# Four chained graph layers on one core: bf16 digits, a tanh, more count buffers and two sweeps reordered

## The reference

```
att   = (q[dst] * kt[edge_type, src]).sum(-1) * mu / sqrt(32)
alpha = segment_softmax(att, dst)
agg   = segment_sum(vt[edge_type, src] * alpha, dst)
out   = typed_linear(gelu(agg), Wa, ba, node_type)      # gelu in its tanh form
x     = a * out + (1 - a) * x
```

## Time and profile before

| | us |
|---|---|
| median of 3 runs | 10061.57 (10060.24 to 10063.58) |
| profiled execution | 10059.76, of which the span is 10058.0 |
| POOL busy | 6847.6 |
| DVE busy | 5828.1 |
| ACT busy | 3071.7 |
| PE busy | 1997.3 |

### The profile page before, as it was taken

One profiled execution on the slowest core, in us unless ns is written; L12 is line 12 of the kernel. 1 busy time (PEld: TensorE's weight loads), 2 busy tenths in 40 slices (PEclk: granted clock), 3 DMA queues, 4 the chain that ended last, 5 costly groups with the idle time before them and its releaser, 6 DMA issues. The chain is left out here.

```text
span 10058.0 us, 59982 instructions
## 1 busy us (share of the span) xinstructions
PE 1997.3 (20%) x16162; PEld 1843.8 (18%) x16162; DVE 5828.1 (58%) x9520; ACT 3071.7 (31%) x3309; POOL 6847.6 (68%) x7186
## 2 busy tenths in 40 slices
PE   4555465651000000002500008000022000110002
PEld 3555465551000000002500007000022000100002
DVE  8777565553545554556588886788874322432225
ACT  6333143331223332232354543355431000110002
POOL 2777777777777777775477763677734777667773
PEclk9999955555555555556855558555555555555556
DMA  3511011111333333334466655566642333223332
GB/s 95 208 29 28 24 44 33 33 31 53 98 99 114 113 109 105 108 110 139 166 212 213 215 183 172 187 217 209 217 124 65 107 103 107 87 90 107 103 107 58
DMA packets 490844, 1161.90 MB, mean 116 GB/s; under 512 B 184121, under 2 KB 279692, under 8 KB 432396
## 3 DMA queue, kind: packets, MB, share of 16 engines
q0 software_dynamic: 255936, 474.70, 18.1%
q1 hardware_dynamic: 204620, 628.82, 16.6%
q10 hardware_dynamic: 29952, 54.54, 2.1%
HBM read 669.61 MB, written 487.92 MB: 115 GB/s over the span
## 5 line engine op out<-in xcount | busy, mean ns | idle before, releaser
L832 POOL DMA_INDIRECT slots<-REC,plc_idx x1664 | 1597.9, 960 | 554.3 <-issue 505.6
L1238 POOL DMA_INDIRECT l_swp_G<-table,KVI x1664 | 1573.3, 945 | 529.1 <-issue 506.3
L940 POOL DMA_INDIRECT l_G<-table,OTHI x1664 | 1581.6, 951 | 513.3 <-issue 506.2
L1490 POOL DMA_INDIRECT l2s_G<-table,OTHI x832 | 785.0, 944 | 428.9 <-issue 253.3
L1490 POOL DMA_INDIRECT l3s_G<-table,OTHI x832 | 786.2, 945 | 301.6 <-issue 253.3
L703 PEld LDWEIGHTS plc_pr<-plc_seen,plc_otf 128*128 128x128 f32 x3328 | 848.4, 325 | 21.3 <-issue 12.1
L703 PE MATMUL plc_pr<-plc_seen,plc_otf 128*128 128x49 f32 x3328 | 849.9, 410 | 11.1 <-DVE plc_seen L618 11.0
L1073 DVE TENSOR_TENSOR l_LB<-l_RE,l_G 128x64 f32<-128x64 f32 x104 | 29.4, 282 | 1024.7 <-DMA l_G<-table,OTHI 1024.5
L1340 DVE SCALAR_TENSOR_TENSOR l_swp_QS<-l_swp_QS,KEEP,l_swp_QX 128x128 f32<-128x128 f32 x1664 | 588.4, 354 | 36.0 <-DMA l_swp_QX<-queries 8.3
L1099 DVE TENSOR_TENSOR_SCAN l_X<-l_AW,l_X 128x2244 f32<-128x2244 f32 x104 | 502.5, 4831 | 3.6
L1399 DVE TENSOR_TENSOR_SCAN l_swp_X<-l_swp_AW,l_swp_X 128x2244 f32<-128x2244 f32 x104 | 501.4, 4821 | 0.1
(11 more groups left out here) (491 smaller groups left out, 9751.1 us busy)
## 6 DMA issues: line engine op xcount, KB each, us to landing
sums<-l_ROW SPq DMA_DIRECT2D x104, 1088.0 KB, 4.3
sums<-l_swp_ROW SPq DMA_DIRECT2D x104, 1088.0 KB
l_swp_QX<-queries SPq DMA_DIRECT2D x104, 1024.0 KB, 7.8
queries<-plc_zrow SPq DMA_DIRECT2D x33, 1664.0 KB
sums<-l3s_ROW SPq DMA_DIRECT2D x52, 1032.0 KB, 4.3
plc_low<-low_rows ACTq DMA_DIRECT2D x208, 256.0 KB, 3.4
sums<-l2s_ROW SPq DMA_DIRECT2D x52, 1024.0 KB, 4.4
table<-t_row SPq DMA_DIRECT2D x98, 512.0 KB
```

What stands on the lines that cost most here:

```text
L832: pool.indirect_dma_start(out=slots, out_offset=bass.IndirectOffsetOnAxis(ap=idx[:, c % IB, j:j + 1], axis=0), in_=g.REC[:, c * CH + j, :] ...
L940: pool.indirect_dma_start(out=G[:, c % GR, j, :], out_offset=None, in_=table, in_offset=bass.IndirectOffsetOnAxis(ap=g.OTHI[:, side(c), x: ...
L1238: pool.indirect_dma_start(out=G[:, c % GR, j, :], out_offset=None, in_=table, in_offset=bass.IndirectOffsetOnAxis(ap=index[:, c * CK + j:c ...
L1490: pool.indirect_dma_start(out=G[:, c % GR, j, :], out_offset=None, in_=table, in_offset=bass.IndirectOffsetOnAxis(ap=g.OTHI[:, k, c * CK + ...
```

## The change

Five things change.

1. The digits are stored as bf16 with the low digits of a key in one run and the high ones in another (`DIG[key, half, column]`), and a f32 copy of the low digits, `LOW`, is kept for ACT and for the transposes. The one-hot tiles are stored with the columns of a chunk interleaved by four, so that the innermost run of `compare` is four neighbours in both inputs and the output. The iota it reads is stored with each value four times (`iota_s` in SBUF, `iota_p` in PSUM). PE and ACT read and write single columns of the tiles with a stride of four values.
2. `count_keys` has 8 buffers, and ACT takes one chunk of four instead of one of three.
3. The gelu is 0.5 x (1 + tanh(z)): Tanh on ACT in the place of Exp, one product on DVE; the 0.5 is put into the weight once.
4. In the attention sweep each half of a chunk's gathers has its own semaphore, and `weigh`, `add_up` and `carry` of the last chunk but one are done in its own iteration.
5. In layer 0's sweep `add_up(c)` and `rows_of(c)` are done in iteration c, behind the pieces of other work.

```diff
+IN = 4
+OB = 8
 def compare(v, out, iota, number):
-    full = [P, out.shape[1], out.shape[2]]
-    return v.tensor_tensor(out, iota.rearrange("p (o w) -> p o w", o=1).to_broadcast(full),
-                           number.to_broadcast(full), ALU.is_equal)
+    full = [P, CH // IN, out.shape[2], IN]
+    return v.tensor_tensor(out, iota.rearrange("p (o w i) -> p o w i", o=1, i=IN).to_broadcast(full),
+                           number.rearrange("p (q o i) -> p q o i", o=1, i=IN).to_broadcast(full), ALU.is_equal)
...
-            v.tensor_copy(down_b[:, :], down[:, 0:1].to_broadcast([P, P]))
+            for to in (cuts, g.iota_s):
+                v.tensor_copy(to[:, 0:IN * P].rearrange("p (w i) -> p w i", i=IN),
+                          g.iota[:, :].rearrange("p (w i) -> p w i", i=1).to_broadcast([P, P, IN]))
...
-                v.tensor_copy(g.DIG[:, k, :, 0], lo[:, :])
-                link(v.tensor_copy(g.DIG[:, k, :, 1], hi[:, :]))
+                v.tensor_copy(g.DIG[:, k, 0, :], lo[:, :])
+                v.tensor_copy(g.LOW[:, k, :], lo[:, :])
+                link(v.tensor_copy(g.DIG[:, k, 1, :], hi[:, :]))
...
+def column(digits, j):
+    return digits[:, j // IN, :, j % IN]
...
-            for c in range(2, NCH, 3):
-                if c >= 3:
-                    act.wait_ge(counted, c - 2)
+            for c in range(3, NCH, 4):
+                if c >= OB:
+                    act.wait_ge(counted, c - OB + 1)
                 for x in range(CH):
-                    o = act.activation(olo[:, 2, x, :], g.iota_b[:, :], ACT.Square, scale=-1.0,
-                                       bias=g.DIG[:, k, c * CH + x, 0:1])
+                    o = act.activation(column(olo[:, c % OB, :, :, :], x), g.iota_b[:, :], ACT.Square, scale=-1.0,
+                                       bias=g.LOW[:, k, c * CH + x:c * CH + x + 1])
...
             for c in range(NCH):
-                if c >= 3:
-                    v.wait_ge(counted, c - 2)
-                if c % 3 < 2:
-                    compare(v, olo[:, c % 3, :, :], g.iota_b[:, :], digit_chunk(g, k, c, 0)).then_inc(low, 1)
-                compare(v, ohi[:, c % 3, :, :], g.iota_b[:, 0:NB], digit_chunk(g, k, c, 1)).then_inc(high, 1)
+                if c >= OB:
+                    v.wait_ge(counted, c - OB + 1)
+                if c % 4 < 3:
+                    compare(v, olo[:, c % OB, :, :, :], g.iota_s[:, :], digit_chunk(g, k, c, 0)).then_inc(low, 1)
+                compare(v, ohi[:, c % OB, :, :, :], g.iota_s[:, 0:IN * NB], digit_chunk(g, k, c, 1)).then_inc(high, 1)
...
-                compare(v, olo[:, c % 2, :, :], g.iota_p[:, :], digit_chunk(g, k, c, 0))
+                compare(v, olo[:, c % 2, :, :, :], g.iota_p[:, :], digit_chunk(g, k, c, 0))
...
-                v.tensor_tensor(hits[:, b, :, :], pr[:, b, 0:CH * NB].rearrange("p (j h) -> p j h", j=CH),
-                                ohi[:, c % HB, :, :], ALU.mult).then_inc(picked, 1)
+                v.tensor_tensor(hits[:, b, :, :].rearrange("p (q i) h -> p q i h", i=IN),
+                                pr[:, b, 0:CH * NB].rearrange("p (q i h) -> p q i h", i=IN, h=NB),
+                                ohi[:, c % HB, :, :, :].rearrange("p q h i -> p q i h"), ALU.mult).then_inc(picked, 1)
...
@@ layer0_sweeps
                 powers(c)
-                if c >= 1:
-                    rows_of(c - 1)
-            rows_of(NC2 - 1)
+                rows_of(c)
...
-            for c in range(NC2 + 1):
-                if c < NC2:
-                    logits(c)
-                if c >= 1:
-                    add_up(c - 1)
+            for c in range(NC2):
+                logits(c)
...
                 if c in directions:
                     add_direction(directions[c])
+                add_up(c)
...
@@ attention_sweep
-                        in_offset=...).then_inc(gathered[c % GR], 16)
+                        in_offset=...).then_inc(gathered[j // QH][c % GR], 16)
...
             def multiply(c, u):
-                v.wait_ge(gathered[c % GR], 16 * CK * (c // GR + 1))
+                v.wait_ge(gathered[u][c % GR], 16 * QH * (c // GR + 1))
...
-            between = {0: (last_maximum, 0), 1: (maximum, 0), 2: (shift, 0), 3: (fall, 0), 4: (cut, 0),
-                       5: (weigh, -1), 6: (add_up, -1), 7: (carry, -1)}
-            for c in range(-1, NCK + 1):
+            front = {0: last_maximum, 1: maximum, 2: shift, 3: fall, 4: cut}
+            close = {5: weigh, 6: add_up, 7: carry}
+            close_now = {QH + 4: weigh, QH + 5: add_up, QH + 6: carry}
+            for c in range(-1, NCK):
                 for x in range(CK):
                     if c + 1 < NCK:
                         query(c + 1, x)
-                        if x == QH - 1:
-                            multiply(c + 1, 0)
-                    if x in between:
-                        step, back = between[x]
-                        if 0 <= c + back < NCK:
-                            step(c + back)
+                    if c >= 0 and x in front:
+                        front[x](c)
+                    if c >= 1 and x in close:
+                        close[x](c - 1 if c < NCK - 1 else c)
+                    if c == NCK - 2 and x in close_now:
+                        close_now[x](c)
+                    if c + 1 < NCK and x == QH - 1:
+                        multiply(c + 1, 0)
...
@@ turn_layer
+            if not closes_l0:
+                v.wait_ge(w_ok, 16)
+                link(v.tensor_scalar(w1[:, :, :], w1[:, :, :], 0.5, None, ALU.mult))
...
-                    link(v.scalar_tensor_tensor(out=sq, in0=sq, scalar=1.0 / c0, in1=x, op0=ALU.add, op1=ALU.mult))
-                    v.tensor_scalar(sq, sq, -2.0 * c * c0, 80.0, ALU.mult, ALU.min).then_inc(ready, 1)
-                elif j == 2:
+                    v.scalar_tensor_tensor(out=sq, in0=sq, scalar=1.0 / C0, in1=x, op0=ALU.add, op1=ALU.mult).then_inc(ready, 1)
+                elif j == 3:
                     v.wait_ge(rooted, G + 1)
-                    link(v.tensor_scalar(sq, sq, 1.0, None, ALU.add))
-                    link(v.reciprocal(sq[:, 0:3, :], sq[:, 0:3, :]))
-                elif j == 3:
-                    link(v.reciprocal(sq[:, 3:GT, :], sq[:, 3:GT, :]))
-                elif j == 4:
-                    v.tensor_tensor(x, x, sq, ALU.mult).then_inc(normed, 1)
+                    v.scalar_tensor_tensor(out=x, in0=sq, scalar=1.0, in1=x, op0=ALU.add, op1=ALU.mult).then_inc(normed, 1)
...
-                        act.activation(SQ[:, G % 2, :, :], SQ[:, G % 2, :, :], ACT.Exp).then_inc(rooted, 1)
+                        act.activation(SQ[:, G % 2, :, :], SQ[:, G % 2, :, :], ACT.Tanh, scale=C1 * C0).then_inc(rooted, 1)
...
-                        g.DIG = sbi("DIG", [P, 2, EC, 2])
+                        g.iota_s = sbi("iota_s", [P, IN * P], BF16)
+                        g.LOW = sbi("LOW", [P, 2, EC])
+                        g.DIG = sbi("DIG", [P, 2, 2, EC], BF16)
```

More of the change, by code:

```diff
@@ L682, in tally_up @@
                 for j in range(CH):
-                    last = pe.matmul(pd[:, j * NB:(j + 1) * NB], olo[:, c % 2, j, :], ohi[:, c % HB, j, :],
-                                     start=True, stop=True)
+                    last = pe.matmul(pd[:, j * NB:(j + 1) * NB], column(olo[:, c % 2, :, :, :], j),
+                                     column(ohi[:, c % HB, :, :, :], j), start=True, stop=True)
                 last.then_inc(tally, 1)
@@ L704, in find @@
                               start=True, stop=False)
[L705 removed]
+                    last = pe.matmul(pr[:, b, j * NB:(j + 1) * NB], bm[:, b, j, :], column(ohi[:, c % HB, :, :, :], j),
                                      start=False, stop=True)
```

68 lines of the change are left out of this document (34 added, 34 removed).

## The result

The changed kernel takes 9951.24 us (median of 4 runs, 9948.50 to 9955.55) against 10062.58 (10060.24 to 10065.57): a ratio of 0.989, interval 0.9872 to 0.9907. The forecast was 9952. Its profiled execution took 9951.04 us, with a span of 9949.3.

The account below looks back on a forecast made before the run. POOL's indirect DMAs were taken to bound the placings and sweeps. Terms 1 − 47 − 3 − 9 − 14 + 0 − 37 = −109 on the profiled 10059.76, median 1.8 above, gave 9952 us; range 9922 to 10000.

Parts of the forecast that it names:

- Where a gain can lie: Only five places can pay: the load, counting, the fills and tails of the POOL-bound stages, and the turns.
- Counting, -47 and +1 for the load: Counting: compares at double rate leave ACT the bound, ending at 118.2 for 165.05, −47 us; extra load work, +1.0 us.
- Rival B: Strided bf16 access is slow on ACT or PE: counting gains only 24 us, total 9975; chance 0.13.
- Fills, -3: Starts of the two placings: double-rate compares shorten the wait before the first scatter, −2.2 and −1.5, taken as −3 us.
- Layer 0, -9.0: End of layer 0's sweep: with add_up in its own iteration, ACT's last powers start at once, −9.0 us.
- Attention, -14: Ends of the two attention sweeps: split halves and an earlier close save 6.9 us each, −14; bodies stay at 20.0.
- Turn 1, 0: Turn 1: its head gets 7 us shorter on DVE, but ACT's wait for the t_qr stores swallows it; 0 us.
- Turn 2, -37: Turn 2: without reciprocals, −5.2 us a group over five groups, head −7.3, second group −4; −37, between −25 and −45.
- A: The double rate of the compares does not engage: counting −3, fills 0, total 9999 us; chance 0.12.
- Squares over 0.45: Sign to watch in counting: ACT's Squares above 0.45 us, where 0.39 was expected, would point to slow strided access.
- C: PE warms in turn 2: a clock of 1.00 lowers the tile floor from 3.16 to 2.3, total 9926 us; chance 0.09.
- D: In the placings, faster compares slow POOL's scatters: +82 by overlapped time, +240 by scatters touched, taken +130; total 10082; chance 0.04.

Follow-up runs that it names:

- e1: Changed kernel with the digits stored as f32 again, same layout and 8 buffers; counting ended at 162.03 us in place of 121.17.
- e2: Changed kernel with counting's old schedule: three buffers, ACT taking every third chunk; counting ended at 173.80 us in place of 121.17.
- b1: The kernel before, unchanged, profiled again on another chip: 10067.57 us, layer 0's sweep body 2227.51 us against 2222.34 in its first profile.
- e5: Changed kernel with layer 0's sweep in its old order, add_up and rows_of one chunk late: 9964.17 us; body 2226.73 (unedited control 2226.23).
- e7: Changed kernel with the attention sweeps as before, one semaphore for all 16 gathers and the late close: 9968.58 us.
- e4b: Changed kernel with the iota of the placings' compares read from SBUF in place of PSUM, on a third chip: 9997.32 us (unedited control 9956.77).

## Why the prediction was right, step by step

- *Where a gain can lie.* Right. The bodies of the placings, of the attention sweeps and of the plain sweeps moved by less than 1.1 us; all of the gain lies in the places that the prediction named.
- *Counting, -47 and +1 for the load.* Right in its mechanism: the double rate (taken without a row that showed it) takes DVE out of the way, and with the buffers ACT no longer waits and is the bound. The term was 2 us too large, because eight Squares with a stride of 8 bytes take 2.64 and not 2.44 us; half of that 0.2 comes back, since the next Squares start 0.97 us after the Relu and not the 1.06 that the sum took, which leaves 26 times 0.1 a cycle. Rival B's price was 0.10 for each Square; 0.2 for eight is a quarter of it. That TensorE's clock would fall to 0.50 in this stage was not foreseen, and cost nothing. e1 and e2 show what the sum did not say: the buffers with f32 digits gain 3 us, bf16 with the old buffers loses 9 (1 of it in the load), both together gain 44.
- *Fills, -3.* Right, 3.2: the first fill gave its 2.2, the second 1.0 where 1.5 was the guess. The Trainium skill was cited with two pages that differ on a compare with one operand in PSUM: "Vector Engine (DVE) Microarchitecture Reference", section Performance modes, grants it the double rate, the tier table of "VectorE: DVE Perf Modes" does not. The rows decide for the first (0.68 us for 1024 with iota in PSUM). e1 agrees with the first page's condition that all operands be 2-byte.
- *Layer 0, -9.0.* Right: 9.0 at the end. The body's +4.3 is no effect of the change (b1, e5).
- *Attention, -14.* Right, 14.3; e7 gives 15.0. In the first sweep the last product starts 0.7 us later after the landing than worked out (5.8 for 5.1), and all behind it too (24.1 for 23.4).
- *Turn 1, 0.* Right as far as the runs can tell: the head's gain went into ACT's wait, as the prediction said, though by less than the 7 us it named. ACT comes to the wait 5.8 us sooner after the first fetch (49.66 for 55.42), the wait is 4.1 longer (15.89 for 11.75), and the fetches are done 1.6 sooner. The 3 us less of the first pair of profiles lie in the spread of the kernel after.
- *Turn 2, -37.* The mechanism was right; in this profile the size is 3.4 too small, over seven profiles with Tanh (203.4 in the mean, against 241.9 in the three with Exp) it is 1.5. Four steady groups gained 20.7 (123.97 to 103.29 us between the same rows of OWN), 5.2 each as worked out. All ahead of them, the head and the groups that run into it, gained 19.8 (78.23 to 58.47 from the first fetch), where 7.3, 4 and one more group of 5.2 make 16.5; the tail did not move (35.03 both). So what was undersized lies in the start of the turn, and there the profiles differ: up to that row the seven with Tanh took 58.5 to 61.4 us, the three with Exp 77.3 to 78.2, a gain of 15.8 to 19.8 around the 16.5.
- *Rivals.* A fell with the rows of the compares. B fell with the Squares' cost of 2.64 us for eight, though by the prediction's own sign ("Squares over 0.45") it would have stood: their mean is 0.56 us, and a mean of operations that overlap was the wrong thing to watch. C fell with the granted clock of 0.50 in turn 2. D was real as a mechanism, and its condition was what kept it out: with one input in PSUM the scatters stayed at 960 ns, with both in SBUF they cost 43.5 us (e4b), half of the lower bound of its price (82). "GPSIMD Engine Reference", Key points, of the Trainium skill names a 2-port mode or two SBUF inputs as the condition for contention, and e4b agrees on the second.

The total agrees to 1 us partly by luck: the errors of +2 (counting), -3.4 (turn 2), -3 (turn 1) and +4.3 (layer 0's body) cancel, and the last two, with part of turn 2, are spread between executions. Runs of the kernel after alone lie between 9948.5 and 9956.8.

## What to carry to other kernels

Where two engines and a buffer share a loop, work out each one's cycle before and after; a faster operation whose engine is not the only bound gains nothing until the split and the buffers move too. Here it even lost, by what its new layout cost the other engine. A producer that runs ahead lets you re-split by the measured cycles, which gave another 18 us here (121.17 to 103.28). In a stage that an issuing engine bounds, look at its first and last chunk: what is queued ahead of the last chunk's work is worth its full length there and nothing in the middle.

## What the runs showed of the hardware

- A compare with two bf16 inputs and a bf16 output in runs of four at step 1 takes 0.68 us for 1024 elements a partition (1.2 with one f32 input), whether the iota is in SBUF or in PSUM; one input was held over the row with a step of 0 on an outer dimension. Whether it needs the runs of four was not tried.
- An indirect DMA of POOL that starts while a DVE operation with two SBUF inputs runs is held until 0.12 us before that operation's end, and then takes its usual 0.94 us (47 gathers beside the operation of 1.09 us; the scatters of e4b within 0.02 us). It is not held where the operation starts after it (34 of 35 gathers), nor where it starts in the first 0.03 us of a compare (e4b).
- With one of the inputs in PSUM nothing is held: the same compare at the same rate leaves the scatters' mean at 960 ns, and in the two attention sweeps of the kernel after 399 gathers start inside scans of 4.82 us, one of whose inputs is in PSUM, and take 945 ns.
- ACT writes bf16 with a stride of 8 bytes at almost its usual rate: a Square of 128 starts 0.300 us after the one before, contiguous 0.292. But each takes 0.565 us to its end in place of 0.386, and an operation that waits for the last one pays that once.
- TensorE's granted clock fell from 1.00 to 0.50 at 47 us in the kernel after, when the counting stage kept PE busier than before (19.26 of 40 us for 11.82), and the whole first placing then ran at 0.50. No figure here shows a cost of it: ACT's cycle and the scatters' mean are the same at either level.
- On one chip the same kernel before took 1417 us more, while counting, which moves hardly any data, agreed across chips (121.3 and 121.4 for the kernel after's 121.2). Before totals or DMA stages are compared across chips, the kernel before has to be timed on each.
